# Linear attention in single steps, with the next stage's queries and last context split at its end

## What is computed

```python
def phi(x): return jax.nn.elu(x) + 1.0
# linear attention, 16 heads of 16; H is x
q, k, v = split(H @ W_qkv.T + b_qkv)             # q, k through phi
state = sum over tokens (phi(k) outer v), ksum   # one state per image and head
o = (phi(q) @ state) / max(phi(q) @ ksum, 1e-6)
o = regroup(o) @ W_proj.T + b_proj               # heads and tokens are interleaved
H = layernorm(2 * H + (layernorm(o) * gamma + beta))
# cross attention, 8 heads of 32; y is the context [4, 1601, 192]
Q, K, V = H @ Wq + bq, y @ Wk + bk, y @ Wv + bv
H = layernorm(H + softmax(Q K^T / sqrt(32)) V @ Wo + bo)
```

## Time and profile before

| | us |
|---|---|
| median of 3 executions | 2863.01 (2862.64 to 2864.55) |
| the profiled execution | 2878.78, span 2877.5 |
| linear stage | 1231 to 1433.6 of the span |
| cross head up to the first pair | 1433.6 to 1512.8 |
| first exponential of the scores | 1514.87 |
| scores and products | 1512.8 to about 1975 |

### The profile page before, as it was taken

The page is one execution under the profiler, slowest core; times in us unless marked ns, Lnnn a source line. Parts: engine busy times, 40 slices in busy tenths (PEclk is TensorE's granted clock), DMA queues, the critical chain, the costliest instruction groups (busy, mean ns, idle before and its releaser), DMA issues. The chain is left out here.

```text
span 2877.5 us, 41419 instructions
## 1 busy us (share of the span) xinstructions
PE 2241.8 (78%) x15582; PEld 1430.9 (50%) x15582; DVE 1720.1 (60%) x3425; ACT 1182.4 (41%) x2185; POOL 592.3 (21%) x488
## 2 busy tenths in 40 slices
PE   6996469898506999378669999996788787788777
PEld 3553137675405888334325555554455544455534
DVE  5676975467783333356646665651777652677663
ACT  2121664334332333033125555554566442566543
POOL 2220000001073445501120000000322142322052
PEclk9997579998657999689779999998899998899989
DMA  3001400100161111232230111102000001000000
GB/s 108 1 1 27 140 1 1 45 1 1 45 219 55 45 50 41 70 91 71 75 98 24 34 25 24 36 13 88 1 1 1 11 0 59 1 1 1 29 19 23
DMA packets 75073, 113.28 MB, mean 39 GB/s; under 512 B 22916, under 2 KB 59744, under 8 KB 74208
## 3 DMA queue, kind: packets, MB, share of 16 engines
q1 hardware_dynamic: 71808, 102.24, 11.9%
q0 software_dynamic: 3072, 8.39, 0.9%
HBM read 85.38 MB, written 31.20 MB: 41 GB/s over the span
## 5 line engine op out<-in xcount | busy, mean ns | idle before, releaser
L2457 DVE TENSOR_REDUCE xa_max<-psum 128x1 f32<-128x1024 f32 (+1 forms) x256 | 248.9, 988 | 144.6 <-PE psum L2360 144.0
L2553 ACT ACTIVATE xa_work<-psum 128x1024 f32<-128x1024 f32 (+1 forms) x208 | 212.9, 1024 | 202.1 <-PE psum L2383 200.4
L2398 PE MATMUL psum<-xa_work,xa_values 128*33 128x128 f32 (+1 forms) x3328 | 232.1, 284 | 0.0
L2398 PEld LDWEIGHTS psum<-xa_work,xa_values 128*33 128x33 f32 (+1 forms) x3328 | 173.0, 114 | 78.8 <-issue 73.7
L2752 PE MATMUL psum<-wqkv_l,x_hl_l 128*128 128x512 bf16 x576 | 147.0, 403 | 61.0 <-POOL x_hl_l L3012 32.1
L3118 PE MATMUL psum<-h_ch_f,w_f 128*128 128x512 bf16 (+1 forms) x576 | 139.2, 399 | 32.5 <-DVE h_ch_f L3178 9.6
L1623 DVE TENSOR_SCALAR moe_raw<-psum,tile_b 128x256 f32<-128x256 f32 x184 | 78.3, 475 | 138.1 <-PE psum L1465 137.0
L2383 PE MATMUL psum<-xa_query_rows,xa_key_rows 98*128 98x512 bf16 (+1 forms) x416 | 131.5, 399 | 8.4 <-ACT xa_work L2553 7.7
L1719 POOL TENSOR_TENSOR x_ch<-moe_raw,x_ch 128x512 bf16<-128x512 f32 x92 | 105.4, 1157 | 151.6 <-ACT x_ch L1679 149.6
L2360 PE MATMUL psum<-xa_key_rows,xa_query_rows 96*128 96x512 bf16 (+1 forms) x512 | 129.3, 348 | 6.7 <-DVE xa_max L2457 3.0
L1465 PE MATMUL psum<-moe_rows,moe_w 128*128 128x256 bf16 x1104 | 132.2, 278 | 3.0 <-POOL moe_rows L1715 3.0
(11 more groups left out here) (435 smaller groups left out, 4929.9 us busy)
## 6 DMA issues: line engine op xcount, KB each, us to landing
xa_key_rows<-cross_keys SPq DMA_DIRECT2D x48, 200.1 KB, 3.5
moe_raw<-in_moe_w SPq DMA_DIRECT2D x16, 512.0 KB, 5.2
x_ch<-in_moe_w SPq DMA_DIRECT2D x16, 512.0 KB, 4.6
moe_rows<-slots_in SPq DMA_DIRECT2D x23, 256.0 KB, 2.8
slots_out<-moe_rows SPq DMA_DIRECT2D x23, 256.0 KB, 2.1
ctx_f<-in_ctxT SPq DMA_DIRECT2D x2, 2401.5 KB, 25.5
cross_keys<-xa_k_hl SPq DMA_DIRECT2D x6, 800.5 KB, 4.8
xa_query_rows<-cross_queries SPq DMA_DIRECT2D x48, 64.0 KB, 3.5
```

The costliest lines, as they stand in the source:

```text
L2398: ins = pe.matmul(total.ap[a * LANE:a * LANE + VC, c:c + PIECE], t["v"][b][0:rows, kt, first + a, :], exps[0:rows, a, c:c + PIECE], start= ...
L2457: v.tensor_reduce(t["maxes"][n % 2][:, qt * HU + a, part:part + 1], u.wide[:, 0:c1 - c0], AX.X, ALU.max).then_inc(*u.free)
L2553: act.activation(t["exps"][k % EXPS][0:rows], u.wide[0:rows].rearrange("p (m q) -> p m q", q=T), ACT.Exp, scale=1.0 / float(np.sqrt(np.flo ...
```

## The change

The linear plan is written in single steps: each query half, key and value tile, read and projection is its own step. `state(b)` now stands ahead of the next image's inputs and `read(b)` behind them and behind `project(b-1)`. Each norm is in two steps: `spread` and `scale` for the first, `close` and `finish` for the second; ScalarE's square root belongs to `spread` and `close`, GpSimd's addition to `scale`. `close` and `finish` follow one image behind. After `channels(b)` of images 0 to 2 stand `x_split`, the two `queries` and `asked`, which were in the cross stage; the query weights are loaded and split with the others. The last nine steps of the plan carry two side steps each, which are those of image 2 and, at the very end, the split of context 3. ScalarE's exponential of a key tile stands ahead of its copy of the value tile. One `q_hl` and one `x_hl` take the place of two each.

The head of the cross stage starts with the loads of three units and two key steps; then come the first 27 maxima with the rest of image 3's keys, its split, values and queries between them. Context, its parts and the query weights stay in SBUF from one stage to the other; the work space of the exponentials is shared with keys, queries and x parts of image 3, so the first exponentials wait for their stores. The waits that the first steps of image 3 had on context and weights are left to `settle`. The engines' functions follow these steps; cut to the core:

```diff
@@ linear_plan
+    def inputs(b):
+        return [("q", b, c) for c in range(HALVES)] + [("kv", b, n) for n in range(TPB)] if b < B else []
+    def project(b):
+        return [("project", b, n) for n in range(TPB)] + [("spread", b)] if b >= 0 else []
+    def close(b):
+        return [("scale", b), ("close", b)] if b >= 0 else []
+    def finish(b):
+        return [("finish", b), ("channels", b)] + ([("x_split", b)] + [("queries", b, c) for c in range(HALVES)] + [("asked", b)]
+                                                   if b < AHEAD else []) if b >= 0 else []
+    plan = inputs(0)
     for b in range(B):
-        plan += [("inputs", b + 1)] if b + 1 < B else []
-        plan += [("state", b), ("read", b)]
-        plan += [("project", b - 1)] if b else []
-        plan += [("regroup", b)]
-        plan += [("channels", b - 3)] if b > 2 else []
-        plan += [("close", b - 2)] if b > 1 else []
-    plan += [("channels", B - 3), ("close", B - 2), ("project", B - 1), ("close", B - 1), ("channels", B - 2), ("channels", B - 1)]
+        plan += [("state", b)] + inputs(b + 1) + project(b - 1) + [("read", b, n) for n in range(TPB)] + close(b - 1)
+        plan += [("regroup", b)] + finish(b - 1)
     side = [("weights",)] + flat([[("parts", b), ("context", b)] + key_steps(b) + value_steps(b) for b in range(AHEAD)])
-    return plan[:2] + mingle(plan[2:], side)
+    side += [("parts", AHEAD), ("context", AHEAD)]
+    end = project(B - 1) + close(B - 1) + finish(B - 1)
+    late = len(side) - 2 * len(end)
+    return plan[:HALVES] + mingle(plan[HALVES:], side[:late]) + flat([[p] + side[late + 2 * n:late + 2 * n + 2] for n, p in enumerate(end)])
@@ linear_attention
         settle(m, [use["channels", B - 1, h].done for h in range(HALVES)] + [use["value", AHEAD - 1, KT - 1].done]
-               + [s.k_stored0.now(), s.k_stored1.now(), s.v_ones.now()])
+               + [s.q_stored.now(), s.a_low.now(), s.b_low.now(), s.k_stored0.now(), s.k_stored1.now(), s.v_ones.now()])
@@ linear_sp
-        elif kind == "context" and b + 1 < AHEAD:
+        elif kind == "context" and b < AHEAD:
@@ linear_dve
         elif kind == "close":
...
-            norm_dve(m, s, nth["close", b], m.x_tok, m.x_tok, group(b))
+            linear_spread(m, s, [m.x_tok[:, i, :] for i in group(b)], b)
+        elif kind == "finish":
+            linear_scale(m, s, [m.x_tok[:, i, :] for i in group(b)], b, nth["close", b])
@@ new functions
+def linear_spread(m, s, tiles, b):
+    v = m.nc.vector
+    for n, i in enumerate(group(b)):
+        ins = v.bn_stats(m.stats[:, i, :], tiles[n])
+    ins.then_inc(*s.v_step.up())
+    v.wait_ge(*s.v_step.now())
+    for i in group(b):
+        ins = v.bn_aggr(m.mv[:, i, :], m.stats[:, i, :])
+    ins.then_inc(*s.variance.up())
+
+def linear_scale(m, s, tiles, b, nth):
+    v = m.nc.vector
+    v.wait_ge(*s.deviation(nth))
+    v.reciprocal(m.rstd[:, TPB * b:TPB * (b + 1)], m.std[:, TPB * b:TPB * (b + 1)]).then_inc(*s.v_step.up())
...
@@ linear_act
-                act.wait_ge(*use["kv", b, n].done)
-                act.copy(t["v_tok"][b % 2][:, n, :, 0:P], kv[:, D:2 * D].rearrange("p (h c) -> p h c", c=P)).then_inc(*s.v_copied.up())
-                act.wait_ge(*s.low(6 * b + 2 + n + 1))
-                act.activation(low[:, 0:D], low[:, 0:D], ACT.Exp).then_inc(*s.raised.up())
+            act.wait_ge(*s.low(6 * b + 2 + n + 1))
+            act.activation(low[:, 0:D], low[:, 0:D], ACT.Exp).then_inc(*s.raised.up())
+            act.wait_ge(*use[step].done)
+            act.copy(t["v_tok"][b % 2][:, n, :, 0:P], kv[:, D:2 * D].rearrange("p (h c) -> p h c", c=P)).then_inc(*s.v_copied.up())
@@ linear_pool
         if kind == "context":
             g.wait_ge(*s.closed.now())
+            g.wait_ge(*s.x_low.now())
             context_pool(m, s, t, b)
-        elif kind == "project":
+        elif kind == "x_split":
+            split_pool(m, s, t, use, b)
+        elif kind == "scale":
             g.wait_ge(*s.scaled(b + 1))
@@ prepare_act (both stages)
+    elif kind == "x_split":
+        b, = step[1:]
...
+        if first == 0:
+            for h in range(HALVES):
+                act.wait_ge(*use["channels", b, h].done)
+        act.copy(t["x_hl"][:, 0], m.x_ch[:, :, b * T:(b + 1) * T]).then_inc(*s.x_high.up())
@@ cross_plan
-    rest = asked(2) + asked(3) + flat([key_steps(b) + value_steps(b) for b in range(AHEAD, B)])
-    plan = asked(0) + [("parts", B - 1), ("context", B - 1)] + asked(1) + mingle(rest, maxima[:lead])
+    rest = key_steps(AHEAD) + [("x_split", AHEAD)] + value_steps(AHEAD) + [("queries", AHEAD, c) for c in range(HALVES)] + [("asked", AHEAD)]
+    plan = rest[:2] + mingle(maxima[:lead], rest[2:])
@@ cross_sp
-    sp.dma_start(t["w_f"][:], dram["xa_q"].rearrange("(h p) o -> p h o", h=2)).then_inc(*s.w_loaded.up(16))
-    context_sp(m, s, t, B - 1)
+    for u in range(3):
+        load(u)
...
+            sp.wait_ge(*s.q_stored(16))
@@ cross_act
             if k >= EXPS:
                 act.wait_ge(*s.multiplied(k - EXPS + 1))
             else:
...
+                act.wait_ge(*s.q_stored(16))
```

More of the change, by code:

```diff
@@ L1808, in linear_sp @@
         kind, b = step[0], step[-1]
-        if kind == "regroup":
+        if kind == "asked":
+            for c in range(HALVES):
+                sp.wait_ge(*use["queries", b, c].done)
+            asked_sp(m, t["q_hl"][:], b).then_inc(*s.q_stored.up(16))
+        elif kind == "regroup":
             oc = t["o_ch"][b % 2]
@@ L1898, in linear_pe @@
         elif kind == "project":
+            n, u = step[2], use[step]
             pe.wait_ge(*loaded[b](16))
-            for n in range(TPB):
-                u = use["project", b, n]
-                pe.wait_ge(*u.empty)
-                for h in range(HALVES):
-                    ins = pe.matmul(u.ap[:, 0:D], t["rg"][b % 2][:, h, n * P:(n + 1) * P], t["wproj"][:, h, :], start=h == 0, stop=h == 1)
-                ins.then_inc(*u.fill)
+            pe.wait_ge(*u.empty)
+            for h in range(HALVES):
+                ins = pe.matmul(u.ap[:, 0:D], t["rg"][b % 2][:, h, n * P:(n + 1) * P], t["wproj"][:, h, :], start=h == 0, stop=h == 1)
+            ins.then_inc(*u.fill)
         elif kind == "channels":
-            pe.wait_ge(*s.normed(TPB * nth["close", b]))
+            pe.wait_ge(*s.normed(2 * b + 2))
             for h in range(HALVES):
@@ L1982, in linear_dve @@
+            ins.then_inc(*u.free)
+        elif kind == "project":
+            n, u = step[2], use[step]
+            v.wait_ge(*u.full)
+            v.tensor_tensor(projected(m, b)[:, n // 2, n % 2, :], u.ap[:, 0:D], m.row("la_bproj"), ALU.add).then_inc(*u.free)
+        elif kind == "spread":
             for n in range(TPB):
                 v.wait_ge(*use["project", b, n].done)
-                v.bn_stats(m.stats[:, TPB * b + n, :], tiles[n]).then_inc(*s.v_step.up())
-            v.wait_ge(*s.v_step.now())
@@ L2035, in linear_act @@
                 act.copy(oc[:, h, :].rearrange("p (s m) -> p s m", s=N0), u.ap.rearrange("p (m s) -> p s m", s=N0)).then_inc(*u.free)
-        elif kind in ("project", "close"):
-            norm_act(m, s, nth[kind, b], group(b))
+        elif kind in ("spread", "close"):
+            tiles = slice(b * TPB, (b + 1) * TPB)
+            act.wait_ge(*s.variance(nth[step]))
+            act.activation(m.std[:, tiles], m.mv[:, tiles, 1], ACT.Sqrt, bias=m.eps[:, 0:1]).then_inc(*s.deviation.up())
         elif kind == "channels":
@@ L2075, in prepare_pe @@
     pe, kind = m.nc.tensor, step[0]
-    if kind == "keys":
+    if kind == "queries":
+        b, c = step[1:]
+        u = use[step]
+        pe.wait_ge(*s.x_low(b - first + 1))
+        pe.wait_ge(*u.empty)
+        for h in range(HALVES):
+            for n, (x, w) in enumerate(PASSES):
+                ins = pe.matmul(u.ap, t["wq"][:, w, h, c * P:(c + 1) * P], t["x_hl"][:, x, h, :],
+                                start=(h, n) == (0, 0), stop=(h, n) == (1, 2))
+        ins.then_inc(*u.fill)
+    elif kind == "keys":
         b, o, c0 = step[1:]
@@ L2148, in prepare_act, with split_pool @@
         act.activation(t["k_hl"][o][:, 0, c0:c1], u.wide[:, 0:c1 - c0], ACT.Identity, bias=m.col("xa_bk", o)).then_inc(*s.in_high.up())
+def split_pool(m, s, t, use, b, first=0):
+    g = m.nc.gpsimd
+    g.wait_ge(*s.x_high(b - first + 1))
+    if b > first:
+        for c in range(HALVES):
+            g.wait_ge(*use["queries", b - 1, c].full)
+    g.tensor_tensor(t["x_hl"][:, 1], m.x_ch[:, :, b * T:(b + 1) * T], t["x_hl"][:, 0], ALU.subtract).then_inc(*s.x_low.up())
 def context_pool(m, s, t, n):
@@ L2180, in cross_plan @@
 def cross_plan():
-    def asked(b):
-        return [("x_split", b)] + [("queries", b, c) for c in range(HALVES)] + [("asked", b)]
     maxima = []
@@ L2277, in rows_loaded @@
     return (s.rows0, s.rows1, s.rows2)[u % 3]
-def asked_stored(s, b):
-    return (s.q_stored0, s.q_stored1)[b % 2]
 def max_loaded(s, u):
@@ L2338, in cross_pe @@
```

(1 more changed line is left out.)

349 lines of the change are left out of this document (144 added, 205 removed).

## The result

The changed kernel takes 2890.99 us (median of 6 executions, 2887.33 to 2897.42), the kernel before on the same chip 2868.87 (6 executions, 2862.64 to 2875.13). The ratio is 1.0080, 95% interval 1.0060 to 1.0101: 0.8% slower, some 22 us (17 to 29). The profiled execution took 2889.15 with a span of 2887.8.

What follows compares the result with a forecast made beforehand. It took serial hand-overs between engines, none of them full, as the bound. VectorE's idle time was to grow 31.3 us in the linear stage and fall 28.5 in the head, +2.8, giving 2866 us (2846 to 2881).

Steps and rivals of the forecast that it cites:

- GpSimd's addition: Norms in two parts: VectorE waits for GpSimd's addition between scale and close, 8.0 us in all, bounds 4 and 10.
- the addition beside the first context's split: During image 1's inputs, VectorE's addition of two SBUF operands waits for GpSimd's split for image 0: +2 us.
- the sum: VectorE's forecast idle time, 104.5 us in the linear stage and 14 in the head; chance 0.42 as it stands.
- the head: Cross attention's start to the first exponential: 46 us instead of 81.3, with 14 us of VectorE idle time, bounds 11 and 22.
- Keys of images 0 and 1: Linear stage: ScalarE's key copies stand behind its input steps, 8 us idle on VectorE, the largest 4.8 at image 1.
- Waits for projections: Regroup round trip through DRAM makes TensorE's projections late on VectorE: 3.9 us for image 2, 2.6 for image 3.
- State: VectorE's state step newly waits for TensorE's state product of 2.05 us: 6.3 for four images, bounds 2 and 9.
- End of stage: Last nine steps with eighteen side steps: 14.4 us idle before spread(3), 5 for context 3's split; bounds 14 and 24.
- Channels and queries: Serial chain after each image's finish in the linear stage leaves VectorE idle 21.5 us, bounds 10 and 27.
- rival B: TensorE at half clock in linear stage chains ending with queries and in last projections: 13 us more, 2879; chance 0.17.
- rival A: Linear stage chains are filled by side steps: queries 10 instead of 21.5, GpSimd's additions 4 instead of 8, 2850; chance 0.32.
- Rival C: In the head, stores, rows and last queries queue on each other, first exponential 8 us later: 2874; chance 0.09.

Runs made afterwards that it cites:

- e1: Changed kernel without the split of x and the queries of images 0 to 2 (zeros stored); linear stage 250.7 us, ratio 1.0063 to the kernel before.
- e13: Changed kernel with side list spread evenly and queries of images 0 to 2 left out, regroup in place; linear stage 234.6 us, ratio 0.9992 to the kernel before.
- e3: Changed kernel with regroup(b) ahead of scale and close of image b-1; linear stage 255.7 us, ratio 1.0080 to the kernel before.
- e2: Changed kernel with its side list spread evenly over the whole plan; linear stage 239.9 us, ratio 1.0035 to the kernel before.
- e12: Changed kernel with side list even, queries of images 0 to 2 left out, regroup ahead of scale and close; linear stage 223.7 us, ratio 0.9961 to before.
- e18: The same kernel as e16, measured again; linear stage 216.8 us, head 49.4, ratio 0.9944 to the kernel before.
- e4: Changed kernel with the queries of each image issued one image later, all work done; linear stage 251.1 us, ratio 1.0077 to the kernel before.
- e7: Changed kernel with regroup ahead of close and scale of image b-1 between image b's reads; linear stage 248.3 us, ratio 1.0067 to before.
- e9: Changed kernel with side list even, and channels, split and queries issued one image later; linear stage 242.2 us, ratio 1.0049 to the kernel before.
- e16: Changed kernel, side list even, queries two images behind, early regroup, scale between reads, six side-step places before last projections; linear stage 218.6 us, ratio 0.9943 to before.
- e17: Changed kernel with side list even and six side-step places between last regroup and last projections; linear stage 243.1 us, ratio 1.0019 to the kernel before.

## Why the prediction was wrong

What held: VectorE's busy time (168.1 for 168.2, part of it chance: 169.7 stood before, of which 4.2 were two instructions stretched beside GpSimd's context splits, and the changed kernel has one, stretched by 2.1); nothing changes behind the first exponential; GpSimd's addition 8.2 (forecast 8.0); queries 15.3 (near 15); `spread(3)` 22 us behind `project(3)` (1428.15 to 1449.95, forecast 22), with keys of image 2 and waits of 9.35 and 3.09 in it; the clock in the stage 0.80 (below 0.87); the addition beside the first context's split: 2.82 against 0.69 for its fellows, ending 0.55 us behind GpSimd's 3.24, which itself was not stretched (3.36 for the other three splits). But I had put its 2 us into the idle time, and they are part of VectorE's busy time.

The idle time was 14.2 us more than the sum: 11.3 in the linear stage, 2.9 in the head. Term by term in the stage:

- Keys of images 0 and 1: 13.5 (26.5 less 13.0 for image 2) where I had 8; values 4.7 where I had nothing, though 7.4 stood before: +10.2, the largest miss. The longest, 5.95 ahead of image 1's first keys, is the one of 6.11 before; I had priced it at 4.8, and taken the value steps for filler that brings no waits.
- Waits for projections 2.5 where I had 6.5: -4.0. The round trip was there, but VectorE's own chain was as long.
- State 8.0 for 6.3, inputs 35.4 for 33.4 (three first queries behind the state, 2.12, 0.95 and 0.88): +3.7. The first state product took 3.81, not 2.05, which is 1.8 of it.
- End of stage 16.3 (13.0 and 3.3 for the last context split) for 19.4: -3.1. Channels and queries 22.4 for 21.5: +0.9.
- 2.9 us of gaps that no row of waits names. They are in the 73.2 of before (the waits listed there sum to 70.0), and my recount by named waits left them out while I compared it with the full 73.2: a plain error of bookkeeping.
- The small rest is square roots, casts, weights and GpSimd's addition, less the 2 us counted for the stretched one: +0.7.

In the head: 51.4 for 46, of which 2.9 idle and 2.5 work. 2.1 of that work are the stretch of before that I had read as idle. Of the idle time values cost 3.3 where I had 0.8, queries 1.9 for 0.6, keys 8.6 for 8.8. ScalarE's first exponential waited 3.92 us for the query store, and the table load behind it took 1.28; VectorE still had maxima then and idled for 2.6 of it, where I had 3.8.

Two sums of the prediction do not come out: the terms of rival B add up to 14, not 13 (three images of 3.0, then 3 and 2), and four `channels` of 1.2 are 4.8, not the 5.5 in the term for channels and queries. Neither changes the verdict.

So the step that failed is the price of the side list. Keys of images 0 and 1 were put at 8 and values at nothing in the linear stage, and values at 0.8 in the head; they measured 13.5, 4.7 and 3.3, which is 12.7 us more, beside smaller misses of both signs (14.2 in all). Why the keys waited 5.5 us longer than I had them is not shown. With it failed rival A's premise, that cheaper queries would bring their price back: e1 shows they would have brought nothing, since another chain, the regroup through DRAM, takes the place of the waits that go.

Rival B's time (2879) was the nearest. Its signs came in part: all four groups of transposes of `channels` took 1.97, the twelve matmuls of image 0's queries 4.18 (six take 1.47 at the granted clock of 1.00 and 2.74 at 0.50), image 2's 2.74 and 1.47, but image 1's ran at full clock (1.47 and 1.45), and TensorE's busy time in both stages rose by 3.6 us only (204.6 to 208.2). Beside the durations that the prediction used (1.09, 1.4 and 2.05) these steps and the first state product took 8 us more on TensorE, an estimate from their rows; but waits for channels and queries came to 22.4 where 21.5 was forecast without B. What the lower clock costs by itself was not tried. It does not set the stage's length alone: at a granted clock of 0.81 the stage took from 234.6 (e13) to 255.7 us (e3). Whether a part of the loss is the clock's stays open. Rival C had the right direction, but only 2.9 of the 5.4 us by which the head was longer are waits, and those are values and queries, not rows or stores.

What the change costs, then, as far as the runs show: 9.5 us from the side list pushed behind the last projections (e2), and 16.2 on the even list from queries and a closing norm put between the reads and the regroup, which show only when both are taken away (e12, which also leaves the queries' own work out). Together they exceed the loss of the whole because the head gave 29.8 back; of the 47.4 us in the linear stage they are 25.7. The other 21.7 (223.7 in e12 against 202.0 before) were traced to no cause; with all the work in it the best order still took 216.8 (e18).

## What to carry to other kernels

Where several engines work down one written order, a wait's total is not what its removal brings: e1, e4, e7 and e9 took away the wait that they aimed at, e3 made the loads earlier, and none shortened the stage by more than the 2 us in which the one repeat differs. Look for the chain that would end next (here the regroup through DRAM) and shorten both, and measure edits in pairs. Do not leave independent work for behind the last round trip: with 27, 3 and 18 side steps ahead of the last regroup, between it and the last projections, and behind, the stage took 249.4 us, with 39, 4 and 5 it took 239.9. The kernel before had 30, 8 and 8. That the work belongs into the round trip itself is less clear: 35, 7 and 6 won only 2.8 us behind the last load.

## What the hardware showed beyond that

The head of the cross stage has the same steps in all the new orders, and its length went with TensorE's granted clock in it: 49.5 us at 0.88 (e12), 53.0 at 0.76 (e16), 55.5 at 0.68 (e13), 59.8 at 0.64 (e17). One kernel had 0.76 in one run and 0.88 in the other (e16, e18). The rest behind the first exponential, with no edit in it, lay between 1348.5 (e12) and 1362.8 us. So for effects below 10 us the stages say more than one profile's span, and the medians of many executions more than either.
